# Two attentions of a four-stage Flamingo-like block: row maxima carried by DMA into the turned queries

## The reference

```python
x = x + tanh(g_xattn[0]) * xattn0(layernorm(x), ctx, ctx)          # 16 heads of 16, no projections
x = x + tanh(g_ffn[0])   * bitlinear_ffn(layernorm(x))
x = x + tanh(g_xattn[1]) * xattn1(layernorm(x), ctx, ctx, Wq, Wk, Wv)  # the same behind relu(x @ W.T)
x = x + tanh(g_ffn[1])   * routed_experts(layernorm(x))

scores = einsum('bqhd,bkhd->bhqk', q, k) * 16 ** -0.5
out = einsum('bhqk,bkhd->bqhd', softmax(scores), v)
```

## Time and profile before

| | us |
|---|---|
| median of 3 runs | 1877.53 (1872.9 to 1878.95) |
| profiled execution, its own time | 1878.45 |
| its span, first to last instruction | 1876.7 |
| mean granted TensorE clock | 0.968 |
| TensorE busy | 1596.0 |
| VectorE busy | 1554.4 |
| ScalarE busy | 1184.8 |
| GpSimd busy | 865.1 |

### The profile page before, as it was taken

One profiled execution on the slowest core, in us unless ns is written; L12 is line 12 of the kernel. 1 busy time (PEld: TensorE's weight loads), 2 busy tenths in 40 slices (PEclk: granted clock), 3 DMA queues, 4 the chain that ended last, 5 costly groups with the idle time before them and its releaser, 6 DMA issues. The chain is left out here.

```text
span 1876.7 us, 49808 instructions
## 1 busy us (share of the span) xinstructions
PE 1596.0 (85%) x20058; PEld 1094.2 (58%) x20058; DVE 1554.4 (83%) x2977; ACT 1184.8 (63%) x1916; POOL 865.1 (46%) x932
## 2 busy tenths in 40 slices
PE   0799999856766766748999999996899999999998
PEld 0577777624444444435777777775466666665665
DVE  7799999857888888876888888886888888888885
ACT  1789889778777787716888888886233333333332
POOL 1455555427777777753333333332233333333332
PEclk9999999979999999969999999998899999999999
DMA  9200000000000000000002000000121211212211
GB/s 313 92 3 3 3 3 3 3 0 1 1 1 1 1 1 1 1 17 2 3 2 70 3 2 3 3 3 1 59 100 58 102 69 57 103 68 71 100 57 68
DMA packets 45526, 68.11 MB, mean 36 GB/s; under 512 B 6273, under 2 KB 36737, under 8 KB 45313
## 3 DMA queue, kind: packets, MB, share of 16 engines
q1 hardware_dynamic: 42944, 65.03, 10.3%
q10 hardware_dynamic: 2368, 0.02, 0.1%
HBM read 56.39 MB, written 8.65 MB: 35 GB/s over the span
## 5 line engine op out<-in xcount | busy, mean ns | idle before, releaser
L719 ACT ACTIVATE a_exp<-a_score_t 128x1024 f32<-128x1024 f32 x256 | 262.1, 1024 | 81.8 <-PE a_score_t L526 81.7
L641 DVE TENSOR_REDUCE a_maxes<-a_score 128x8 f32<-128x1024 f32 x256 | 311.2, 1216 | 0.6 <-PE a_score L509 0.6
L1547 POOL TENSOR_TENSOR e_a_parts<-e_act,e_a_parts 128x512 f16<-128x512 f32 x128 | 153.3, 1198 | 329.1 <-ACT e_a_parts L1518 329.1
L1518 ACT ACTIVATE e_a_parts<-e_act 128x512 f16<-128x512 f32 x128 | 80.6, 630 | 303.0 <-DVE e_act L1350 269.0
L1095 POOL TENSOR_TENSOR b_hidden<-b_hidden,b_shifted 128x508 f32<-128x508 f32 x128 | 161.6, 1262 | 119.3 <-DVE b_hidden L945 119.3
L1232 PE MATMUL e_up_ps<-e_n_turned,e_up_t 128*128 128x512 f16 x768 | 187.9, 381 | 8.5 <-DVE e_act L1346 8.5
L1246 PE MATMUL e_out<-e_down_t,e_a_parts 128*128 128x256 f16 x1536 | 188.4, 273 | 0.8 <-POOL e_a_parts L1547 0.8
L1232 PE MATMUL e_gate<-e_n_turned,e_gate_t 128*128 128x512 f16 x768 | 187.9, 381 | 0.2 <-issue 0.2
L1246 PEld LDWEIGHTS e_out<-e_down_t,e_a_parts 128*128 128x128 f16 x1536 | 149.6, 98 | 39.0 <-POOL e_a_parts L1547 1.1
L1102 POOL TENSOR_TENSOR b_hidden<-b_hidden,b_scales 128x512 f32<-128x512 f32 x128 | 168.2, 1318 | 3.0 <-ACT b_scales L1077 3.0
L780 POOL TENSOR_TENSOR a_split<-ctx,a_split 128x256 f16<-128x256 f32 x64 | 43.0, 672 | 268.6 <-ACT a_split L736 268.6
(11 more groups left out here) (206 smaller groups left out, 4027.5 us busy)
## 6 DMA issues: line engine op xcount, KB each, us to landing
ctx<-e_weights SPq DMA_DIRECT2D x64, 512.0 KB, 5.4
out<-x SPq DMA_DIRECT2D x16, 512.0 KB, 2.9
x<-in_x SPq DMA_DIRECT2D x3, 2048.0 KB, 19.0
ctx<-in_ctx SPq DMA_DIRECT2D x1, 4096.0 KB, 27.0
ctx<-in_ctx SPq DMA_DIRECT2D x1, 3072.0 KB, 16.5
a_exp<-in_L_ffn_w SPq DMA_DIRECT2D x2, 1024.0 KB, 9.6
x<-in_x SPq DMA_DIRECT2D x1, 1536.0 KB, 16.4
ctx<-in_ctx SPq DMA_DIRECT2D x1, 1024.0 KB, 13.5
```

What stands on the lines that cost most here:

```text
L641: nc.vector.tensor_reduce(maxes[:, p * PAIRS:(p + 1) * PAIRS], score[:, :].rearrange("p (h k) -> p h k", k=P), AX.X, ALU.max).then_inc(max ...
L719: nc.scalar.activation(exp32[:, u % 2, 2 * p:2 * p + 2, :], score_t[:, :].rearrange("p (g n) -> p g n", g=2), ACT.Exp, scale=DH ** -0.5 / ...
L1547: nc.gpsimd.tensor_tensor(a_parts[:, e % 4, 1, :], act3[:, e % 2, :], a_parts[:, e % 4, 0, :], ALU.subtract).then_inc(alo_ok, 1)
```

## The change

In both attentions the 8 matmuls with `spread` of each transposed pass are left out, and the mask is neither made nor stored. Instead the turned maxima go into a row of `q_turned` that had held zeros: partition 48 for the first of two heads and 112 for the second. The keys' row against it holds the constant `unit`: -1 in attention 0, the scale of the scores in attention 1. Product and sum then contain the subtraction.

TensorE turns 16 columns of maxima in place of 128. VectorE copies them to `neg_max_t` as before (now 16 partitions), and SyncE, which waits for that copy, issues two DMAs per tile, one of 8 partitions of 256 bytes for each half. Each half has semaphores of its own for even and odd tiles.

The passes are exchanged: slot 1 of a step now computes and exponentiates pass 1 of the tile before (lag EL + 1), slot 2 pass 0 of the present tile (lag EL), and this pass waits for the two DMAs. Otherwise the order of work on each engine stays.

In attention 0 the maxima are written as float16 straight into `neg_max`, and the negation (L693) goes; in attention 1 it stays. The experts' weights are loaded in 27 pieces, one behind each pair of DMAs of the tiles 32 to 58, in place of a burst.

```diff
+FIRST_PIECE = 32
+MOVED = (True, True)
...
+    moved = MOVED[layer]
+    unit = scale * scale if layer else -1.0
+    passes = ((EL + 1, 1), (EL, 0)) if moved else ((EL, 0), (EL, 1))
...
-        neg_max = sb("neg_max", [P, 2, 2, SLOT], F16)
-        neg_max_t = sb("neg_max_t", [P, 2, P], F16)
+        neg_max = sb("neg_max", [P, 2, 2, PAIRS if moved else SLOT], F16)
+        neg_max_t = sb("neg_max_t", [HEADS if moved else P, 2, P], F16)
+        largest = lambda u: neg_max[:, u % 2, :, 0:PAIRS].rearrange("p r (a k) -> p a r k", k=HG)
...
-            nc.vector.memset(k_stack[:, :, :, 3, 0:1], 1.0).then_inc(made, 1)
+            nc.vector.memset(k_stack[:, :, :, 3, 0:1], unit if moved else 1.0).then_inc(made, 1)
...
+            @block.sync
+            def _(sp):
+                def step(t, u):
+                    if moved:
+                        sp.wait_ge(m_copied, t + 1)
+                        for half in range(2):
+                            row = half * SLOT + 3 * DH
+                            sp.dma_start(q_turned[row:row + 1, u % 4, :, :],
+                                         neg_max_t[half * PAIRS:(half + 1) * PAIRS, u % 2, :]).then_inc(max_in[half][u % 2], 16)
+                    if layer and t >= FIRST_PIECE:
+                        if t == FIRST_PIECE:
+                            sp.wait_ge(cl_ok, 3 * EXPERTS)
+                        load_experts(nc, sp, io, m, t - FIRST_PIECE)
+
+                write_steps(step, UNROLL, TILES, 0)
...
                 def do_scores_t(t, u, p):
-                    if p == 0:
+                    if p == 0 and moved:
+                        for half in range(2):
+                            reach(pe, max_in[half][u % 2], 16 * (t // 2 + 1))
+                    elif p == 0:
                         reach(pe, m_copied, t + 1)
                     reach(pe, exp_ok, t * 2 + p)
...
-                        for half in range(2):
+                        for half in range(0 if moved else 2):
                             h, _ = head_of(2 * p + half, k)
                             r = SLOT * half
                             last = nc.tensor.matmul(score_t[:, column(half, k)], spread[r:r + SLOT, h // 2, :],
...
+                    def scores_t_pass(n):
+                        lag, p = passes[n]
+                        if inside(i - lag, TILES):
+                            do_scores_t(i - lag, (u - lag) % UNROLL, p)
...
-                    if run_exps:
-                        do_scores_t(i - EL, uE, 0)
+                    scores_t_pass(0)
...
-                    if run_exps:
-                        do_scores_t(i - EL, uE, 1)
+                    scores_t_pass(1)
...
-                        take_max(i - SL, 1)
+                        take_max(i - SL, uS, 1)
+                    if layer and run_scores:
                         reach(dve, max_ok, (i - SL) * 2 + 2)
```

More of the change, by code:

```diff
@@ L361, in attention_stage @@
         score, score_t = banks("score"), banks("score_t")
-        spread = sb("spread", [P, PAIRS, P], F16)
+        if not moved:
+            spread = sb("spread", [P, PAIRS, P], F16)
         spread_made = sem("spread_made")
         def make_spread(pool):
-            nc.gpsimd.memset(spread[:], scale * scale).then_inc(spread_made, 1)
+            if moved:
+                return
+            nc.gpsimd.memset(spread[:], unit).then_inc(spread_made, 1)
             pool.wait_ge(spread_made, 1)
@@ L408, in attention_stage @@
         q_copied, k_copied, m_copied = sem("q_copied"), sem("k_copied"), sem("m_copied")
+        max_in = [[sem(f"max_in{half}_{n}") for n in range(2)] for half in range(2)]
         scores_ok, max_ok, neg_ok = sem("scores_ok"), sem("max_ok"), sem("neg_ok")
@@ L475, in attention_stage @@
         with nc.Block() as block:
[L477 to L482, removed]
+            @block.sync
+            def _(sp):
+                def step(t, u):
+                    if moved:
+                        sp.wait_ge(m_copied, t + 1)
[8 more added lines that the diff above has]
+                write_steps(step, UNROLL, TILES, 0)
+                if layer:
+                    for loaded in m.expert_loaded[0:3]:
+                        sp.wait_ge(loaded, 16 * EXPERTS)
+                    sp.wait_ge(m.expert_loaded[3], 48)
             heads = lambda ap: ap.rearrange("p (h d) -> p h d", h=HEADS)
@@ L520, in do_scores_t @@
                             r = SLOT * half
-                            nc.tensor.matmul(score_t[:, column(half, k)], k_turned[r:r + SLOT, u % 4, h // 2, :],
-                                             q_turned[r:r + SLOT, u % 4, h // 2, :], start=True, stop=False)
-                        for half in range(2):
+                            last = nc.tensor.matmul(score_t[:, column(half, k)], k_turned[r:r + SLOT, u % 4, h // 2, :],
+                                                    q_turned[r:r + SLOT, u % 4, h // 2, :], start=True, stop=moved)
+                        for half in range(0 if moved else 2):
                             h, _ = head_of(2 * p + half, k)
@@ L722, in step, with exp_pass @@
                 def step(i, u):
-                    run_exps = inside(i - EL, TILES)
-                    uE = (u - EL) % UNROLL
+                    def exp_pass(n):
+                        lag, p = passes[n]
+                        if inside(i - lag, TILES):
+                            do_exp(i - lag, (u - lag) % UNROLL, p)
                     if not layer and isinstance(i, int) and i in (0, head - 1):
@@ L748, in step @@
                         nc.scalar.activation(k_turned[:, (u - TL) % 4, :, :], k_bank[:, :].rearrange("p (n k) -> p n k", k=P), ACT.Copy).then_inc(k_copied, 1)
-                    if run_exps and not layer:
-                        do_exp(i - EL, uE, 1)
+                    if not layer:
+                        exp_pass(1)
                     if not layer and inside(i, TILES):
```

63 lines of the change are left out of this document (35 added, 28 removed).

## The result

The changed kernel takes 1907.55 us (median of 4 runs, 1905.15 to 1913.07), the kernel before 1878.24 us on the same chip. The ratio is 1.0163, with a 95% interval of 1.0148 to 1.0179. The forecast of 1867.5 us had the wrong sign, and its range ended at 1903. The profiled execution took 1908.72 us with a span of 1907.0, which is 30.3 us more than the span before. Its mean granted clock was 0.969 (before 0.968).

What follows compares the result with a forecast made beforehand. Attention 0 was held by TensorE's in-order loop with its wait for the maxima's copy; attention 1 had TensorE always busy. Profiled 1878.45 - 6.8 - 6.2 + 3.0 = 1868.5 us, so a 1867.5 us forecast; range 1850 to 1903.

Steps and rivals of the forecast that it cites:

- G: Attention 0, start of VectorE's copy of the maxima to start of slot 2: taken as 2.12 us, range 2.05 to 2.25.
- (e): Attention 0: two added DMAs per tile make a new loop, 0.65 + G + 1.96 = 4.73 us a step, gaining 6.8 us.
- Rival 2: Attention 0: the DMA wait replaces the removed one and is longer, landing 2.1 us, step 5.30; 1903 us, chance 0.30.
- (a): Attention 0: 8 of 16 matmuls go per transposed pass, 0.22 us, leaving 1.96 us from slot 2 to next scores.
- (b): Attention 0, slot 1: it does the older tile's pass 1, so its 0.46 us wait for the maxima goes.
- (c): Attention 0: the 0.17 us negation leaves VectorE, which gives nothing by itself.
- Rival 3: Attention 1 isn't held by VectorE and takes the 27 us, attention 0 at 4.73: 1847 us, chance 0.04.
- Rival 4: TensorE, pausing some 0.7 us before slot 2, is granted a clock below 1.00: 17 us, so 1885 us, chance 0.05.
- The ends: Fill and drain of each attention: one uncovered DMA round trip, between 0 and 8 us in all, taken as 3.
- (d): Attention 0: queries are turned early and VectorE's idle before copying them goes; VectorE alone would allow 4.51 us a step.
- rival 1: Attention 0: the DMA round trip is shorter, G below 1.90, VectorE binds at a 4.51 us step; 1853 us, chance 0.18.
- the split copy: Attention 1: VectorE's 0.69 us copy holds the turn of the queries, limiting the gain to 0.10 us a step, 6.2 us.

Runs made afterwards that it cites:

- one-half kernel: Changed kernel with attention 0 issuing and awaiting only the first half's DMA per tile, the second half's maxima left out: 1875.39 us in one run.
- wide kernels: Changed kernel with both attentions' transposed passes one step later and maxima turned from 128 columns: 1867.72 us; with attention 0's normalising moved earlier too: 1849.15 us.

## Why the prediction was wrong

**The failing step** is the term G in (e), the price of the DMA pair. Its parts, forecast and measured: copy to issue 0.25 and 0.24 us; first issue with its gap 0.34 and 0.67; start of the second issue to slot 2, 1.46 by the row (1.53 in the 2.12 taken) and 1.75. The time from the end of an issue to the semaphore was right: 1.46 - 0.28 = 1.18 us in the earlier trace rows, 1.75 - 0.63 = 1.12 here. It was the issue that was mis-sized, twice over, since the two stand one behind the other: 0.33 us in the first and, with a landing 0.06 shorter, 0.29 in the second. I had taken the row that "the transfer is like in all but its target", and the target made the difference (0.634 against 0.282 us with everything else equal). G became 2.66 where the break-even was 2.23, and the rest of the loop was right to 0.07 us: (2.66 - 2.12) - 0.07 = 0.47 us more than 4.73 is the 5.20 measured. In all 62 x 0.47 = 29 us, on a margin of 0.11 us a step. The row was read rightly, but it stands for a transfer with another kind of target.

**Rival 2** (0.30) came nearest in its time, 1903, and in what it said of attention 0, where the wait takes the place of the old one and is longer. Its mechanism was another: it had the landing at 2.1 us and the issue at 0.34, two errors that cancel to 0.03 us of G, so that its closeness is luck. The Trainium skill's 2.0 us (DMA: Bandwidth & Descriptors, Anatomy of one DMA) gave 5.20 us in the prediction, which is what was measured, but by parts that don't hold: it was put beside an issue of 0.34, and the rows have 0.67 and 1.75. A lone DMA in the one-half kernel has 1.72 us from its issue to slot 2. The same page's warning about two transfers to disjoint partition halves (Rules for kernel authors) points the right way: issued at once on two queues they take 2.01 us where one alone takes 1.72. That the shared engines are the reason, no run here shows.

**Right, point by point.** (a) 8 matmuls fewer leave 1.95 us from slot 2 to the next scores (1.96). (b) Slot 1 no longer waits. (c) The negation is worth nothing (4.83 with it gone). Rival 3 is out: attention 1 is held by VectorE at 6.71 and doesn't take 27 us. Rival 4 is out for the regular waits of 0.9 us, with the clock at 1.00 in attention 1 and, but for two stretches, in attention 0; these two, behind tiles 4 and 32, make the 0.99 there and cost some 2.4 us, an estimate from the lengths of those steps. The experts' pieces hold up nothing: steps with a piece are 6.81 like those without, late ones aside. The ends, put down at 3 us, cost 1.9 in attention 0 and at most 1.3 in attention 1.

**Wrong beside G.** (d) VectorE's bound of 4.51 us took its instructions at the lengths they had in their old places. Moved against GpSimd's, one of them grew by 0.27, and the bound is 4.74 to 4.75. At G = 1.96 and with G hidden the step was the same, so rival 1 with its 1853 us could not come about by a faster DMA alone. In attention 1 the step was to fall by 0.10 us through the split copy, and that chain is real (6.71 in the wide kernels); but "the turn of 16 rows in place of 128 ... unchanged" was wrong, and 0.10 us of it took the gain, 6.2 us. The late steps, of which I had nothing, exceed the median by 5.2 and 3.5 us, where the kernel before has 3.2 (in its fill and, by 0.15 to 0.2, once in eight steps) and nothing. In the chances, 0.02 of the 0.19 for no change comes from no term that the text names.

**Account of the 30.3 us** of span: attention 0 23.5 from the step, 2.0 more from late steps, 1.9 from the ends (0.3 ahead of the first copy and 1.6 behind the last), -0.4 the rest; attention 1 0 from the step, 3.5 late steps, 1.3 the rest; the stage between -1.8; others +0.3. The -1.8 and the small rests were not traced.

**The range** reached 4.5 us too low. Rival 2's price was cut at one landing time, and the bounds of G (2.05 to 2.25) were taken from issue rows of DMAs with one end in DRAM. The router's 0.367 to 0.576 us stood next to them and would have spoken for a wider range of the first issue too.

## What to carry to other kernels

A small DMA in a loop-carried chain costs its issue, one for each transfer on the queue, and its landing; take both from a row with the same kind of ends, and if there is none, hide it a whole step away rather than measure the margin in tenths. Put two instructions of VectorE and GpSimd side by side only after looking who starts first: re-read an engine's bound with the lengths of its new neighbours. A shape that a change makes smaller needs a row of its own as much as a wait that it adds.

## What the runs showed of the hardware that was not expected

- The issue of a DMA of 8 x 256 bytes by SyncE takes 0.634 us with both ends in SBUF and one partition as its target (0.624 us with eight), and 0.282 us with its target in DRAM; ScalarE's issue of the first takes 0.637. From the end of the issue to the waiting engine's start it is about 1.1 us in either case that was read closely (0.634 case 1.12, one half 1.09).
- Two such issues at once on two queues: 0.63 and 0.64 us each, and 2.01 us to the waiting engine.
- A weight load of 128 columns starts 0.15 us behind the start of one of 16 columns, and 0.02 behind one of 128.
- VectorE's normalising of 128x256 float32 takes 0.40 us alone and 0.67 beside a GpSimd instruction that began 0.15 us earlier; if VectorE begins first, GpSimd's takes 0.82 in place of 0.67.
- Nine of 128 pairs of DMAs land 0.2 to 2.2 us late in the kernel after, each with a packet of kind "instruction" (8 or 16 KB) in transfer beside it; 34 of the 119 others have one too.
- Behind two of TensorE's long waits in attention 0 (1.9 us ahead of 83.61 and of 232.04) the granted clock fell to its lower level; behind waits of 1.99 us in attention 0 and 2.06 us in attention 1 it did not.
